# A four-stage transformer block: weight buffers released per part, the second attention written out, and the passage into the feed-forward reordered

## What is computed

```python
x = x + tanh(g_xattn[0]) * attention0(layernorm(x), ctx)        # one head of 256; q, k, v share one W and b
x = x + tanh(g_ffn[0])   * sum_e (silu(ln(x) @ Wg[e]) * (ln(x) @ Wu[e])) @ Wd[e]   # 8 experts, 256 -> 1024 -> 256, dense
x = x + tanh(g_xattn[1]) * attention1(layernorm(x), ctx, mask)  # norm twice, 8 heads of 64, Wq, Wkv, Wout
x = x + tanh(g_ffn[1])   * moe(layernorm(x))                    # 8 experts 256 -> 256, best expert, capacity 256 each
```

## Time and profile before

| | us |
|---|---|
| runs | 1377.47, 1388.63, 1392.26 |
| median | 1388.63 |
| profiled execution | 1381.46 |
| its span, first to last instruction | 1379.6 |
| PE / PE weight loads / DVE / ACT / POOL busy | 1268.5 / 1011.2 / 910.8 / 627.9 / 499.5 |
| mean granted clock of PE | 0.979 |

### The profile page before, as it was taken

One profiled execution on the slowest core, in us unless ns is written; L12 is line 12 of the kernel. 1 busy time (PEld: TensorE's weight loads), 2 busy tenths in 40 slices (PEclk: granted clock), 3 DMA queues, 4 the chain that ended last, 5 costly groups with the idle time before them and its releaser, 6 DMA issues.

```text
span 1379.6 us, 18833 instructions
## 1 busy us (share of the span) xinstructions
PE 1268.5 (92%) x6162; PEld 1011.2 (73%) x6162; DVE 910.8 (66%) x1654; ACT 627.9 (46%) x1320; POOL 499.5 (36%) x501
## 2 busy tenths in 40 slices
PE   6979999999999999999999999999999999989945
PEld 4758777777777777777777777777777757767744
DVE  4886676666666666677666666666667647667533
ACT  2444444454444454444444445445444434443510
POOL 2342443333333344444333333344444003233324
PEclk9979999999999999999999999999999999999968
DMA  4040000100000000000100000000000321011033
GB/s 125 24 146 0 24 23 32 38 24 24 24 24 24 24 24 24 23 24 24 40 30 24 24 23 24 23 24 24 23 24 1 107 80 34 32 65 47 19 119 119
DMA packets 46646, 54.42 MB, mean 39 GB/s; under 512 B 4445, under 2 KB 42386, under 8 KB 46431
## 3 DMA queue, kind: packets, MB, share of 16 engines
q1 hardware_dynamic: 41360, 42.92, 9.6%
q0 software_dynamic: 3088, 9.76, 1.9%
q10 hardware_dynamic: 2111, 0.63, 0.2%
HBM read 37.35 MB, written 12.62 MB: 36 GB/s over the span
## 4 chain that ended last, share of the span: by engine, by line
PE 58%; POOL 29%; DVE 4%; issue 4%; ACT 2%; DMA 2%; DVEq 0%; POOLq 0%; ACTq 0%; SPq 0%
PE bank L896 16%; PE bank L897 15%; PE bank L898 15%; POOL w_lo L467 5%; POOL wd_lo L473 4%; POOL w_lo L469 3%; POOL w_raw L453 3%; POOL w_lo L471 2%; POOL w_hi L455 2%; POOL w_hi L465 2%; PE bank L1071 2%; POOL w_raw L452 2%; POOL w_raw L461 2%; POOL w_raw L457 2%; PE bank L1091 1%
## 5 line engine op out<-in xcount | busy, mean ns | idle before, releaser
L896 PE MATMUL bank<-xop_hi,w_hi 128*128 128x512 f32 x896 | 356.3, 398 | 48.0 <-POOL wd_lo L473 38.3
L897 PE MATMUL bank<-xop_lo,w_hi 128*128 128x512 f32 x896 | 353.3, 394 | 0.0
L898 PE MATMUL bank<-xop_hi,w_lo 128*128 128x512 f32 x896 | 352.2, 393 | 0.0
L1451 DVE TENSOR_TENSOR acc<-bank,acc 128x512 f32<-128x512 f32 x248 | 170.7, 688 | 186.1 <-PE bank L898 185.9
L896 PEld LDWEIGHTS bank<-xop_hi,w_hi 128*128 128x128 f32 x896 | 169.5, 189 | 100.6 <-issue 58.8
L452 POOL TENSOR_TENSOR w_raw<-raw_gu 128x256 f32<-128x256 f32 x32 | 23.7, 742 | 600.9 <-PE bank L898 600.9
L897 PE MATMUL bank<-hid_lo,wd_hi 128*128 128x512 f32 x512 | 203.0, 396 | 0.0
L896 PE MATMUL bank<-hid_hi,wd_hi 128*128 128x512 f32 x512 | 202.4, 395 | 0.7 <-DVE hid_lo L1437 0.7
L898 PE MATMUL bank<-hid_hi,wd_lo 128*128 128x512 f32 x512 | 201.3, 393 | 0.0
L898 PEld LDWEIGHTS bank<-xop_hi,w_lo 128*128 128x128 f32 x896 | 169.4, 189 | 38.2
L897 PEld LDWEIGHTS bank<-xop_lo,w_hi 128*128 128x128 f32 x896 | 169.7, 189 | 36.9
(11 more groups left out here) (188 smaller groups left out, 1701.4 us busy)
## 6 DMA issues: line engine op xcount, KB each, us to landing
raw_gu<-in_L_ffn_Wg_dram SPq DMA_DIRECT2D x32, 256.0 KB, 2.7
raw_gu<-in_L_ffn_Wu_dram SPq DMA_DIRECT2D x32, 256.0 KB, 3.1
raw_d<-in_L_ffn_Wd_dram SPq DMA_DIRECT2D x32, 256.0 KB, 3.7
slots<-empty_row POOLq DMA_DIRECT2D x1, 4112.0 KB
kept<-slots SPq DMA_DIRECT2D x8, 258.0 KB, 4.8
x_res<-in_x_dram SPq DMA_DIRECT2D x4, 512.0 KB, 5.3
we_raw<-in_L_ffn_W_dram SPq DMA_DIRECT2D x8, 256.0 KB, 4.3
out_dram<-x_res SPq DMA_DIRECT2D x4, 512.0 KB
```

Source lines behind the costliest of these rows:

```text
L896: mm(ps, w, a, start=start, stop=False, skip_group_check=True)
L897: mm(ps, w, a_low, start=False, stop=False, skip_group_check=True)
L898: return mm(ps, w_low, a, start=False, stop=True, skip_group_check=True)
L1451: nc.vector.tensor_tensor(out=to, in0=ps, in1=to, op=ALU.add).then_inc(acc_added, 1)
```

## The change

- **Release.** `split(q)` becomes `split_hi(q)` and `split_lo(q)`. The gate and up buffers may be written when the last `product4` on "u" of quarter q-2 is done (`p4_ps`), and are ready at `gu_ready`; the down buffers are written last, after all downs of quarter q-2, and are ready at `wd_ready`, for which PE waits ahead of the first down product of a quarter, and SP ahead of a load.
- **Order.** Groups 0 to 3 are (quarter, pair) = (0, 0), (1, 0), (0, 1), (1, 1); from group 4 on as before. Pair 1 is first used by group 2, quarter 1 by group 1.
- **Passage.** The instructions of ACT, PE, DVE and POOL between the first attention and group 2 are reordered as the diff shows. `split_hi(1)` and `split_lo(1)` come early on POOL, with the powers between them; the sums and lo parts of pair 1 go from DVE to POOL. The fill of `slots` goes to SP, behind the fifth load of weights.
- **Second attention.** All loops are written out; `yc`, `kcur`, `vcur` and their copies go, `acc`, `k1T` and `V1` are used in place. The mask and ones rows exist on all partitions, and the two mask matmuls use rows 0 and 32. The experts' loops are written out too (PE, ACT, DVE).

The core of the diff (the same loop and semaphore edits on other engines are left out):

```diff
+        def quarter(n):
+            return n % PAIRS if n < 2 * PAIRS else n // PAIRS
+
+        def pair(n):
+            return n // PAIRS if n < 2 * PAIRS else n % PAIRS
+
+        def groups_through(q):
+
+            return max(n for n in range(GROUPS) if quarter(n) <= q) + 1
+
+        def first_of_pair(n):
+            return n < 2 * PAIRS and quarter(n) == 0
...
+        X_ORDER = (X_11, X_T1, X_T2, X_21, X_T3, X_22, X_T4)
+
+        def x_sum(alu, p, to, a, b):
+            raw = xop_raw[p]
+            alu.tensor_tensor(out=raw[:, to, :], in0=raw[:, a, :], in1=raw[:, b, :],
+                              op=ALU.subtract).then_inc(x_sum_ready[p], 1)
+
+        def x_first_sum(alu, eng, p):
+
+            eng.wait_ge(x_raw_ready, 4 * p + 3)
+            x_sum(alu, p, X_T1, X_T3, X_11)
+
+        def x_other_sums(alu, eng, p):
+
+            eng.wait_ge(x_raw_ready, 4 * p + 4)
+            eng.wait_ge(x_sum_ready[p], 1)
+            x_sum(alu, p, X_T2, X_22, X_T1)
+            x_sum(alu, p, X_T3, X_22, X_T3)
+            eng.wait_ge(x_sum_ready[p], 2)
+            x_sum(alu, p, X_T4, X_21, X_T2)
+
+        def x_sums(alu, eng, p):
+            x_first_sum(alu, eng, p)
+            x_other_sums(alu, eng, p)
+
+        def x_lo_out(alu, eng, p, i):
+
+            s = X_ORDER[i]
+            eng.wait_ge(x_sum_ready[p], 4)
+            eng.wait_ge(x_hi_ready[p], i + 1)
+            alu.tensor_tensor(out=xop_lo[p][:, s, :], in0=xop_raw[p][:, s, :],
+                              in1=xop_hi[p][:, s, :].bitcast(F32), op=ALU.subtract).then_inc(x_lo_ready[p], 1)
...
-                    sp.wait_ge(w_ready, q - 1)
+                    sp.wait_ge(wd_ready, q - 1)
...
+                if q == 4:
+                    sp.wait_ge(empty_ready, 1)
+                    sp.dma_start(slots.rearrange("(n p) r -> p n r", p=P),
+                                 empty_row[:].unsqueeze(1).to_broadcast([P, NT, ROW])).then_inc(slots_empty, 16)
+
+            sp.wait_ge(wd_ready, NQ)
...
-            def expert_sums(f):
-                if not isinstance(f, int) or f > 1:
-                    sp.wait_ge(c_yT_ps, 2 * f)
-                sp.dma_start(yc[:], acc[:, :, bass.ts(f, CH)]).then_inc(y_in, 16)
-
-            def keys_and_values(chunk):
-                b = batch_of(chunk)
-                wait_if(sp, c_sim_ps, 2 * CT * chunk)
-                sp.dma_start(kcur[:], k1T[:, :, bass.ts(b, KEYS)]).then_inc(kcur_in, 16)
-                wait_if(sp, c_o_ps, CT * chunk)
-                sp.dma_start(vcur[:], V1[:, bass.ts(b, 2), :]).then_inc(vcur_in, 16)
...
-                    pool.wait_ge(down_ps, 4 * PAIRS * (q - 1))
+                    pool.wait_ge(p4_ps["u"], groups_through(q - 2))
...
-                nc.gpsimd.tensor_copy(wd_hi[i][:], d[:])
...
+                                        op=ALU.subtract).then_inc(gu_ready, 1)
+                if q >= 2:
+                    pool.wait_ge(down_ps, 4 * groups_through(q - 2))
+                nc.gpsimd.tensor_copy(wd_hi[i][:], d[:]).then_inc(wd_hi_ready, 1)
+                pool.wait_ge(wd_hi_ready, q + 1)
                 nc.gpsimd.tensor_tensor(out=wd_lo[i][:], in0=d[:], in1=wd_hi[i][:].bitcast(F32),
-                                        op=ALU.subtract).then_inc(w_ready, 1)
+                                        op=ALU.subtract).then_inc(wd_ready, 1)
 
             for u in range(NC):
                 power(u, CT, 1)
             split(0)
-            for u in range(NC):
-                power(u, CT, 2)
+            power(0, CT, 2)
             nc.gpsimd.memset(empty_row[:, R_TOKEN].bitcast(U32), DROPPED).then_inc(empty_ready, 1)
-            pool.wait_ge(empty_ready, 1)
-            pool.dma_start(slots.rearrange("(n p) r -> p n r", p=P), empty_row[:].unsqueeze(1).to_broadcast([P, NT, ROW])).then_inc(scattered, ZEROED)
-            for q in range(1, NQ):
+            split_hi(1)
+            power(1, CT, 2)
+            pool.wait_ge(a_ln2, 2)
+            split_lo(1)
+            power(2, CT, 2)
+            power(3, CT, 2)
+            x_sums(nc.gpsimd, pool, 1)
+            for i in range(7):
+                x_lo_out(nc.gpsimd, pool, 1, i)
+            for q in range(2, NQ):
...
-            for u in range(NC):
+            for u in range(NC - 1):
                 a_exps(u)
                 a_pT_out(u)
                 if u + 2 < NC:
                     a_xnT_out(u + 2)
-                if u >= 2:
-                    x_raw_out(u - 2)
+            x_raw_out(0)
+            a_exps(NC - 1)
+            x_raw_out(1)
+            x_hi_first(0)
+            a_pT_out(NC - 1)
             nc.scalar.activation(s11[0:1, 0:1], tg[0:1, 0:1], ACT.Silu)
-            x_hi_out(0)
+            x_hi_rest(0)
...
+                if n == 1:
+                    x_hi_first(1)
...
+                silu_sum(n, "12", half12, sum12)
+                silu_psum(n, "21", s21, bank[FORK_BANK["g"]], p4_ps)
                 if n == 0:
                     x_raw_out(3)
-                silu_sum(n, "12", half12, sum12)
-                if n == 0:
-                    x_hi_out(1)
-                silu_psum(n, "21", s21, bank[FORK_BANK["g"]], p4_ps)
+                if n == 1:
+                    x_hi_rest(1)
...
-                wait_if(pe, a_res, u)
                 for j in range(CT):
+                    if u > 0 and j % 2 == 0:
+                        pe.wait_ge(a_res, 2 * u - 1 + j // 2)
...
-                if u >= 2:
-                    x2_transposes(u - 2)
+                if u == 2:
+                    x2_transposes(0)
                 if u + 1 < NC:
                     a_scores(u + 1)
+                if u == 2:
+                    x2_transposes(1)
...
-                q, p = n // PAIRS, n % PAIRS
-                if n < PAIRS:
-                    pe.wait_ge(x_hi_ready, 7 * p + X_ORDER.index(x) + 1)
-                    pe.wait_ge(x_lo_ready, 7 * p + X_ORDER.index(x) + 1)
+                q, p = quarter(n), pair(n)
+                if first_of_pair(n):
+                    pe.wait_ge(x_hi_ready[p], X_ORDER.index(x) + 1)
+                    pe.wait_ge(x_lo_ready[p], X_ORDER.index(x) + 1)
                 if p == 0:
-                    pe.wait_ge(w_ready, q + 1)
+                    pe.wait_ge(gu_ready, q + 1)
...
+                if pair(n) == 0 and part == 0:
+                    pe.wait_ge(wd_ready, quarter(n) + 1)
...
-                if n == 0:
-                    x2_transposes(NC - 2)
                 product2(n, "g")
                 down(n - 1, 0)
                 product2(n, "u")
                 down(n - 1, 1)
+                if n == 0:
+                    x2_transposes(NC - 2)
                 product7(n, "g")
...
+                if n == 0:
+                    x2_transposes(NC - 1)
...
-                for s in banks:
-                    mm(bank[s][:, 0:HPB * KEYS], ones_r[:], mask_row, start=True, stop=False)
+                for i, s in enumerate(banks):
+                    row = slice(32 * i, 32 * i + 1)
+                    mm(bank[s][:, 0:HPB * KEYS], ones_r[row, :], mrow[row, b, :, :].rearrange("p a k -> p (a k)"), start=True, stop=False)
...
-                    pe.wait_ge(y_in, 16 * f)
-                    y_transposes(yc, 0, (0, 1))
+                    y_transposes(acc, f * CH, (0, 1))
...
             ln2_variances(1)
+            ln2_normed(1)
             a_maxes(3)
-            ln2_normed(1)
-            a_add(2)
+            a_coefs(2)
+            a_add_half(2, 0)
+            x_first_sum(nc.vector, dve, 0)
+            a_add_half(2, 1)
             ln2_variances(2)
-            x_sums(0)
+            x_other_sums(nc.vector, dve, 0)
+            for i in range(2):
+                x_lo_out(nc.vector, dve, 0, i)
             ln2_normed(2)
+            for i in range(2, 4):
+                x_lo_out(nc.vector, dve, 0, i)
             a_add(3)
+            for i in range(4, 7):
+                x_lo_out(nc.vector, dve, 0, i)
             ln2_variances(3)
-            x_lo_out(0)
-            ln2_normed(3)
...
             for n in range(GROUPS + 1):
                 sum_22(n, "g")
+                if n == 0:
+                    ln2_normed(3)
                 sum_12(n, "g")
+                if n == 0:
+                    sum_22(n, "u")
                 hid_psum(n, "11", bank[SUM_BANK["u"]], s11, p2_ps)
-                if n == 0:
-                    x_sums(1)
-                sum_22(n, "u")
+                if n > 0:
+                    sum_22(n, "u")
                 add_up(n - 1, 1)
                 sum_12(n, "u")
                 hid_sum(n, "22", half22, sum22)
                 hid_sum(n, "12", half12, sum12)
-                if n == 0:
-                    x_lo_out(1)
...
-            with dve.Fori(0, E // EB) as p:
+            for p in range(E // EB):
```

More of the change, by code:

```diff
@@ L256, in flamingo_kernel @@
         sd = Arena(nc, xop_at, xop_end)
-        yc = sd.take("yc", [P, KB, CH], F32)
         xnC = sd.take("xnC", [P, CT, D], F32)
@@ L261, in flamingo_kernel @@
```

(16 more changed lines are left out.)

112 lines of the change are left out of this document (44 added, 68 removed).

## The result

The changed kernel takes **1323.43 us** (median of four runs, 1322.35 to 1324.02), the kernel before 1384.11 in the same session; the ratio is 0.9574, with a 95% interval of 0.9531 to 0.9618. Five more runs in another session gave 1322.57 us and 0.9571 (0.9554 to 0.9588). The profiled execution after has a span of 1321.4 us, 58.2 less than before, at the same mean granted clock (0.979).

A forecast was written before the change was run, and what follows sets the result against it. Bound: a circle of PE and POOL's weight split, pausing PE each quarter; second, the passage into the feed-forward. 1381.5 less 45.0 + 15.4 + 5 + 4 = 69.4 gives 1312.1, plus 3 carried over: 1315 us, range 1298 to 1336.

The forecast's parts named there:

- part 2: Start of the feed-forward: reordered passage brings group 2 to 96.2 instead of 111.63; 15.4 us, bounds 5 and 19.
- part 4: Experts: written-out loops remove ACT and DVE idle time, 16 scatters in one row; 4.0 us, bounds 0 and 4.
- part 1: Feed-forward: releasing and awaiting weight buffers per part removes 30 pauses of 1.5 us; 45.0 us, bounds 0 and 45.
- the carry: Whole kernel: 3 us added for the median of runs lying 7.2 us above the profiled execution.
- the start of the gate and up part: POOL's split: starts 4.2 us earlier, at 606.0, ending by 617.0, 4.6 us before PE wants it.
- Rival A: Feed-forward: the pause moves as split and DVE's hidden low parts disturb each other; half 1337, all 1360; chance 0.10.
- bound of 19 us: Passage into the feed-forward: upper bound of its gain, with both groups at their 26.4 us.
- Part 3: Second attention: second mask row runs beside the first on another row group; 5 us, 7.7 at best, 0 at worst.
- D: Feed-forward: slower than before, POOL blocking four DVE instructions ahead of the first low part; 1429 us, chance 0.03.
- B: Passage gains only its start, because unit 3 or pair 1's parts on POOL come late; 1325 us, chance 0.15.
- C: Second attention and experts give nothing: mask matmuls don't overlap, ACT and DVE idle for another cause; 1324, chance 0.12.
- clock near 1.0 from 67 on: Passage: sign that PE starts the feed-forward without idle time ahead, so no matmuls at 1.2 GHz behind it.

The follow-up runs named there:

- r1: Changed kernel, but from quarter 3 on the split again starts only behind the down projections of quarter q-2; 1317.6 us, 0.9546.
- r2: As r1, and PE also waits for the wd part at the head of each quarter from quarter 3 on; 1368.1 us, 0.9934.
- p2: Changed kernel with POOL's low parts of quarter 1 cut in three, placed where DVE reads PSUM or waits; 1319.6 us, 0.9565.
- c1: p2 plus filler transposes at two of PE's waits in each chunk of the second attention; 1316.3 us, 0.9560.
- c2: c1 with the experts' loops of ACT, PE and DVE back, as in the kernel before; 1316.1 us, 0.9565.

## Why the prediction came out as it did

The forecast was 1315 in a range of 1298 to 1336, the result 1323.4; 69.4 us were summed, 58.2 came. Of the 11.2 that are missing 3.1 are part 2's, 6.3 the second attention's (5 forecast, -1.3 in the traces) and 1.9 part 4's; part 1 gave 0.1 more than forecast. The 3 us of the carry, which did not exist, took that much off the miss: luck.

*Part 1: right in size and cause, wrong in one step.* 45.0 forecast, 45.1 in the trace, quarters of 30.47, POOL off the chain. r1 and r2 show that the waiting of PE for wd carried it. The step that failed is the start of the gate and up part: the text put the last `product4` six products before the last down, 4.2 us. It is a whole group and more: product4 of a group stands at that group's end, its downs reach into the second group behind. The split started at 586.38, 19.3 us before the wd part, and the slack is 19.8 us, not 4.6. It cost nothing here, since even r1's slack of 0.8 us is enough. Rival A had its ground: the low parts of the hidden blocks are disturbed more than before (first line before, second after), yet PE waits 0.7 us for them in all, as before:

```profile
L1437 DVE TENSOR_TENSOR hid_lo<-hid,hid_hi 128x512 fp32r<-128x512 f32 x256 | 173.7, 699 | 30.9 <-ACT hid_hi L669 30.9
```
```profile
L1479 DVE TENSOR_TENSOR hid_lo<-hid,hid_hi 128x512 fp32r<-128x512 f32 x256 | 214.8, 860 | 34.5 <-ACT hid_hi L718 34.5
```

*Part 2: the mechanism right, 3.1 us short.* Group 2 came at 99.31, not 96.2. The bound of 19 us was mis-added: both groups at their 26.4 us behind a start at 67.4 give 17.8. The predicted steps inside hold: `ln2_normed(3)` 1.38 us, the transposes of unit 2 and product7's wait (1.22, forecast 1.3), no wait for pair 1 from POOL. From `product1(0)` to group 2 it is 28.7 us, forecast 28.8 (28.4 to 29.6 in the six traces with this order). All of the miss is the start, 70.65 for 67.4. The prediction placed `split_lo(1)` at 56 to 63 and asked only what the other half would do to `ln2_normed(0)` (2.70 us instead of 1.38, hidden). It didn't ask which DVE instructions lie at 56 to 63: `nmsA` and `coefA`, four columns wide, each held up to the end of a POOL instruction of 2.36 and 1.26 us. p2 takes this away, and `product1(0)` starts at 67.01 and group 2 at 96.30, the forecast. The trace before already held the sign of it, an instruction of the same size at `split(0)`:

```profile
38.41 2.33 DVE L1327 TENSOR_SCALAR coefA<-rdenA,tg 128x4 f32<-128x4 f32 x1
```
```profile
38.36 2.35 POOL L467 TENSOR_TENSOR w_lo<-w_raw,w_hi 128x1024 fp32r<-128x1024 f32 x1
```

The prediction cited the Trainium skill, SBUF — State Buffer (SBUF: two separate sides), for instructions with two SBUF inputs only. `nmsA` has one; the same rule also names DVE's two-port modes. The trace agrees with its lock for a whole instruction, taken by whichever starts first: POOL's starts at 56.89, `nmsA` at 57.62, and it takes 1.66 us beside POOL, 0.17 alone. That `nmsA` runs in such a mode, no run shows. The prediction's own are of this kind too: the 7.75 us of `ln2_normed(3)` are four TENSOR_SCALARs with one large input.

*Part 3: mis-sized, and then lost.* 5 us taken; 0.69 to 0.00 a chunk measured, 1.7 in all. From mask to scores 0.34 us are left, not 0.24: the second mask row runs beside the first for 0.14 of its 0.24 us. PE is busy 1.0 us less a chunk, and the chunk at most 0.69 shorter. Waits take up the rest. Of the two readings of the Trainium skill, TensorEngine Tiling (Array Packing), Key Properties, that the prediction set side by side (7.7 us or nothing), neither fits. The stretches at half clock then took more than that in the compared pair.

*Part 4: wrong.* 4.0 forecast. The step that failed: the idle time behind the turn of the loop was taken for the loop's effect, from one execution. Written out, the 16 scatters are not in one row either; they pause for 1.06 and 2.09 us where the kernel before paused for 4.25. Of this the two traces show 2.1 us in the rest behind the last projection, but the changed kernel's rest alone is 57.1 and 58.4 in two executions, so the 2.1 can be scatter. c1 and c2 differ by 0.1 us there, on a chip without the idle time. Its cause stays open.

*The carry.* 3 us were added from the profiled execution to the median. They didn't exist after: 1323.19 and 1323.43.

In terms of the rivals: A and D didn't happen. B did not either: the passage gained 12.3 us, of which its start is 1.6. Of C, the mask rows gave little (1.7 of 5 us), and the cause of the idle time at the experts was another, as it says. The sign "clock near 1.0 from 67 on" did not come true.

## What to carry to other kernels

When a buffer is released and refilled in one piece, ask which part the bound engine waits for: one wait moved from the whole to the part gave 45 of 58 us here, the earlier start nothing as long as the part was ready 0.8 us ahead. When work is moved on POOL, list DVE's instructions at the new place, the tiny ones first, and follow what each of them releases. An idle time seen once, behind a loop's turn or elsewhere, is no term of a sum until executions on more than one chip have it at the same place.
